# A two-part LSTM step reordered on TensorE and VectorE, the SSM's output product in four full-width pieces, and the SSM's input products dealt out 12, 11, 11, 2

## The reference, cut to what matters

```python
h = tanh(x[:, t] @ Wx + b + h @ Wh)                      # layer 0, for each t: x = x + h
B, C = softplus(conv(x) @ Wp[:, :64] + .), tanh(conv(x) @ Wp[:, 64:] + .)   # layer 1
u = x @ Ws + bs
state = decay * state + dt * B * u                       # for each t
x = x + (C * state) @ Wo + bo
A = x[:, t] @ Wx + b + h @ Wh                            # layer 2, for each t; Wh is 512 x 2048
i, f, o = sigmoid(A[:512]), sigmoid(A[512:1024]), sigmoid(A[1024:1536]); g = tanh(A[1536:])
c = f * c + i * g
h = o * tanh(c)                                          # x = x + h
x = x + x @ layer                                        # layer 3
```

## Time and profile before

| | |
|---|---|
| median of 3 runs | 4203.66 us (4202.13 to 4208.72) |
| profiled execution, its own time | 4200.99 us |
| span of its trace | 4199.2 us |
| PE busy | 3705.6 us (88%) |
| DVE busy | 3546.8 us (84%) |
| ACT busy | 1392.5 us (33%) |
| POOL busy | 782.9 us (19%) |
| granted TensorE clock, mean | 0.991 |

### The profile page before, as it was taken

How to read it: one execution, slowest core, us unless ns; L and a number is a source line. 1 busy time by engine, 2 the same in 40 slices (tenths; PEclk the granted TensorE clock), 3 DMA queues, 4 the chain that set the end, 5 groups by cost and what they waited for, 6 DMA issues and landing times.

```text
span 4199.2 us, 260237 instructions
## 1 busy us (share of the span) xinstructions
PE 3705.6 (88%) x111058; PEld 3068.5 (73%) x111058; DVE 3546.8 (84%) x21169; ACT 1392.5 (33%) x6196; POOL 782.9 (19%) x3625
## 2 busy tenths in 40 slices
PE   6989999989999899998989989898999989988866
PEld 4677777777777777777777777777777777777654
DVE  5588888888888888888888888888888888888865
ACT  4233333333333333333333333333333333333221
POOL 0111111112111111111111111111111111111111
PEclk9999999999999999999999999999999999999998
DMA  7100000000000000000000000000000000000000
GB/s 257 46 7 7 10 9 9 9 7 7 9 9 9 9 6 6 9 9 9 9 6 7 8 9 9 9 9 6 7 9 9 9 9 6 6 7 7 6 5 7
DMA packets 19102, 63.37 MB, mean 15 GB/s; under 512 B 3958, under 2 KB 4526, under 8 KB 14914
## 3 DMA queue, kind: packets, MB, share of 16 engines
q1 hardware_dynamic: 17692, 46.67, 3.5%
q10 hardware_dynamic: 294, 0.33, 0.0%
HBM read 38.48 MB, written 8.39 MB: 11 GB/s over the span
## 4 chain that ended last, share of the span: by engine, by line
DVE 46%; PE 35%; ACT 12%; issue 7%; DMA 1%; DVEq 0%; SPq 0%; ACTq 0%; POOL 0%; POOLq 0%
PE ps_lstm L995 26%; DVE lstm_sums L731 13%; DVE lstm_arg L737 9%; DVE lstm_h_scaled L760 5%; ACT lstm_gates_2c L487 5%; ACT lstm_tanh_c L492 4%; DVE rnn_h_parts L873 3%; DVE lstm_gates_2c L748 3%; DVE rnn_arg L837 2%; PE ps_rnn L1034 2%; DVE lstm_h_parts L764 2%; DVE lstm_h_parts L768 2%; DVE rnn_h_parts L875 2%; ACT rnn_h L504 2%; PE ps_lstm_in_b L1076 2%
## 5 line engine op out<-in xcount | busy, mean ns | idle before, releaser
L995 PE MATMUL ps_lstm<-lstm_Wh_parts,lstm_h_parts 128*20 128x256 f16 x65472 | 1993.3, 274 | 444.2 <-DVE lstm_h_parts L768 414.2
L995 PEld LDWEIGHTS ps_lstm<-lstm_Wh_parts,lstm_h_parts 128*20 128x20 f16 x65472 | 1499.9, 91 | 910.6 <-DVE lstm_h_parts L768 687.8
L487 ACT ACTIVATE lstm_gates_2c<-lstm_arg 128x32 f32<-128x32 f32 x2048 | 469.6, 229 | 1677.0 <-DVE lstm_arg L737 1677.0
L731 DVE STREAM_TRANSPOSE lstm_sums<-ps_lstm 128x256 f32<-128x256 f32 x2048 | 914.1, 446 | 114.4 <-PE ps_lstm L995 84.9
L348 POOL COPY lstm_sums<-lstm_in 128x32 f32<-128x32 f32 x2048 | 427.1, 211 | 1820.2 <-DVE lstm_arg L737 1813.4
L1034 PE MATMUL ps_rnn<-rnn_Wh_parts,rnn_h_parts 128*20 128x128 f16 x32736 | 641.3, 220 | 36.7 <-DVE rnn_h_parts L875 36.0
L737 DVE TENSOR_REDUCE lstm_arg<-lstm_sums 128x32 f32<-128x96 f32 x2048 | 538.1, 263 | 105.5
L1034 PEld LDWEIGHTS ps_rnn<-rnn_Wh_parts,rnn_h_parts 128*20 128x20 f16 x32736 | 550.6, 92 | 74.1 <-DVE rnn_h_parts L875 55.6
L492 ACT ACTIVATE lstm_tanh_c<-lstm_gates_2c 128x8 f32<-128x8 f32 x2048 | 410.5, 200 | 353.7 <-DVE lstm_gates_2c L748 353.6
L504 ACT ACTIVATE rnn_h<-rnn_arg 128x16 f32<-128x16 f32 x1024 | 221.6, 216 | 752.2 <-DVE rnn_arg L837 752.2
L873 DVE TENSOR_SCALAR rnn_h_parts<-rnn_h 128x16 f16<-128x16 f32 x1024 | 226.4, 221 | 240.5 <-ACT rnn_h L504 239.1
(11 more groups left out here) (182 smaller groups left out, 2740.8 us busy)
## 6 DMA issues: line engine op xcount, KB each, us to landing
layer_plus_2I<-in_L_cond_w SPq DMA_DIRECT2D x16, 1024.0 KB, 5.3
out<-out_rows SPq DMA_DIRECT2D x128, 64.0 KB, 1.9
x_rows<-in_x SPq DMA_DIRECT2D x31, 256.0 KB
lstm_Wx<-in_L_cond_Wh SPq DMA_DIRECT2D x1, 4096.0 KB, 17.3
lstm_Wx<-in_L_cond_Wx SPq DMA_DIRECT2D x1, 4096.0 KB, 13.8
layer_plus_2I<-in_L_cond_Wh SPq DMA_DIRECT2D x1, 1024.0 KB, 8.4
rnn_Wx<-in_L_cond_Wx SPq DMA_DIRECT2D x1, 1024.0 KB, 10.8
lstm_in<-in_L_cond_w SPq DMA_DIRECT2D x1, 1024.0 KB, 9.7
```

The costliest lines, as they stand in the source:

```text
L487: A.activation(gate[h][:, 0:G, :].rearrange("p g q -> p (g q)"), arg[h][:, :, :].rearrange("p g n -> p (g n)"), ACT.Tanh, scale=gate_scale ...
L731: return mark(V.transpose(tr[h][s % 2][:, :, 0:QC], psL[h][:, 0:HW].rearrange("p (g c) -> p g c", c=QC)))
L995: ins = mm(psL[h][QC * j:QC * j + LO + NB, 0:HW], hls[:, k, :], whl[:, k, h, e, j, :], start=(k == 0 and e == 0), stop=(k == KB - 1 and e ...
```

## The change

In the LSTM step TensorE issues products(1, 0), which needs half 0 of the state alone, in front of its wait for lstm_h_ready1 and in front of products(0, 2) and (0, 3). VectorE's order for one step becomes T0, R0, [SSM piece], T1, P0, R1, C0, O0, TR, P1, H0, A0, C1, B0, O1, A1, H1, RR, B1, [SSM piece], L873, L875. The vector y gets its own zero-padded place for all four sequences (y, 128 x 128), cleared once by GpSimd instead of the two halves of wo2, and is made by two instructions on 64 partitions each; the product with Wo is 4 matmuls of 128 columns. SSM_CUTS deals the 36 products out as 12, 11, 11 and 2.

```diff
--- before.py
+++ after.py
@@ -49,7 +49,7 @@
 HALO_STEP = 14
 OUT_STEPS = [4, 10, 11, 28]
 SSM_MMS = [("u", TAPS - 1, b) for b in range(KB)] + [(c, k, b) for c in "BC" for k in range(TAPS) for b in range(KB)]
-SSM_CUTS = [0, 8, 20, 32, 36]
+SSM_CUTS = [0, 12, 23, 34, 36]
 EXP_STEP = 2
 SERIES_STEP = 3
 CT_STEP = 5
@@ -175,10 +175,11 @@
         o_s = [sb(f"lstm_o_scaled{h}", [P, HB * NB]) for h in range(NH)]
         tc = [sb(f"lstm_tanh_c{h}", [P, HB * NB]) for h in range(NH)]
 
-        zabs, zmax, ez, den, rden, sr, qr, bt, ct, drive, y, pol_a, pol_b, st_ = [
-            stage[:, 3 * 512 + HS * q:3 * 512 + HS * (q + 1)] for q in range(14)]
+        zabs, zmax, ez, den, rden, sr, qr, bt, ct, drive, pol_a, pol_b, st_ = [
+            stage[:, 3 * 512 + HS * q:3 * 512 + HS * (q + 1)] for q in range(13)]
         wpk = stage[:, 6 * 512:10 * 512].rearrange("p (k b c) -> p k b c", k=TAPS, b=KB)
-        wo2 = stage[:, 10 * 512:12 * 512].rearrange("p (h d) -> p h d", h=2)
+        wo2 = stage[:, 10 * 512:11 * 512]
+        y = stage[:, 11 * 512:11 * 512 + TOK].rearrange("p (t n) -> p t n", n=NB)
         states = st_.rearrange("p (t n) -> p t n", n=2)
         st0 = sb("state0", [P, 2])
         spw = sb("softplus_work", [P, 9, 2])
@@ -269,7 +270,7 @@
             sp.dma_start(wp[:, :, :], rows(Wp)).then_inc(d_ssm, 16)
             sp.dma_start(ws[:, :, :], rows(Ws)).then_inc(d_ssm, 16)
             for h in range(2):
-                sp.dma_start(wo2[NS * h:NS * (h + 1), h, :], Wo[:, :]).then_inc(d_ssm, 16)
+                sp.dma_start(wo2[NS * h:NS * (h + 1), :], Wo[:, :]).then_inc(d_ssm, 16)
             sp.dma_start(whl32[:, :, :], rows(l2_Wh)).then_inc(d_lstmw, 16)
             for q in range(W2BUFS - 1):
                 load_w2(q)
@@ -319,10 +320,8 @@
             nc.gpsimd.affine_select(out=ident[:, :], in_=ident[:, :], compare_op=ALU.not_equal, fill=1.0, base=0,
                                     pattern=[[-1, P]], channel_multiplier=1).then_inc(q_id, 1)
             pool.wait_ge(q_id, 2)
-            nc.gpsimd.memset(wo2[NS:P, 0, :], 0.0).then_inc(q_id, 1)
+            nc.gpsimd.memset(y, 0.0).then_inc(q_id, 1)
             pool.wait_ge(q_id, 3)
-            nc.gpsimd.memset(wo2[0:NS, 1, :], 0.0).then_inc(q_id, 1)
-            pool.wait_ge(q_id, 4)
             pool.wait_ge(rmax, 1)
             nc.gpsimd.partition_all_reduce(wmaxa[:, 0:1], wmax[:, 0:1], P, RMAX).then_inc(rmax_all, 1)
 
@@ -751,17 +750,19 @@
                 def out_gate(h):
                     return mark(V.tensor_scalar(o_s[h][:, :], gate[h][:, 2, :], 1.0, H_SCALE, ALU.add, ALU.mult))
 
-                def new_h(h, s, o_at):
+                def tanh_done(h, s, o_at):
 
                     vec.wait_ge(S[f"lstm_tanhc{h}"], s + 1)
                     vec.wait_ge(S["vec_done"], o_at)
-                    o3 = o_s[h][:, :].rearrange("p (b n) -> p b n", b=HB)
-                    t3 = tc[h][:, :].rearrange("p (b n) -> p b n", b=HB)
-                    at = mark(V.tensor_tensor(half(hl, h)[:, :, s, :], o3, t3, ALU.mult))
-                    return at, o3, t3
-
-                def hi_part(h, o3, t3):
-                    return mark(V.tensor_tensor(half(hls, h)[:, :, 0:NB], o3, t3, ALU.mult))
+
+                o3 = [t[:, :].rearrange("p (b n) -> p b n", b=HB) for t in o_s]
+                t3 = [t[:, :].rearrange("p (b n) -> p b n", b=HB) for t in tc]
+
+                def h_part(h, s):
+                    return mark(V.tensor_tensor(half(hl, h)[:, :, s, :], o3[h], t3[h], ALU.mult))
+
+                def hi_part(h):
+                    return mark(V.tensor_tensor(half(hls, h)[:, :, 0:NB], o3[h], t3[h], ALU.mult))
 
                 def lo_part(h, s, at):
                     vec.wait_ge(S["vec_done"], at)
@@ -809,8 +810,13 @@
                         vec.wait_ge(S["vec_done"], m_p[0])
                         vec.wait_ge(S["ct_ready"], 1)
                         mark(V.tensor_copy(st0[:, :], states[:, CT - 1, :]))
-                        V.scalar_tensor_tensor(out=y, in0=st_, scalar=spt[:, 1:2], in1=ct, op0=ALU.mult, op1=ALU.mult
-                                               ).then_inc(S["y_ready"], 1)
+                        if known == 1:
+                            vec.wait_ge(q_id, 3)
+                        for h in range(2):
+                            own = slice(NS * h, NS * (h + 1))
+                            V.scalar_tensor_tensor(out=y[own, :, 2 * h:2 * h + 2], in0=states[own], scalar=spt[own, 1:2],
+                                                   in1=ct.rearrange("p (t n) -> p t n", n=2)[own], op0=ALU.mult, op1=ALU.mult
+                                                   ).then_inc(S["y_ready"], 1)
 
                 def series(out_, in_, c, x_):
 
@@ -848,23 +854,26 @@
                             ssm_stage(s, 0)
                         at = transpose(1, s)
                         p_at = products(0, s)
-                        o_at = out_gate(0)
                         reduce(1, s, at)
                         new_cell(0, p_at)
+                        o_at = out_gate(0)
                         if w["rnn"]:
                             r_at = transpose_rnn(s)
                         p_at = products(1, s)
-                        _, o3, t3 = new_h(0, s, o_at)
+                        tanh_done(0, s, o_at)
+                        h_part(0, s)
+                        at = hi_part(0)
                         new_cell(1, p_at)
-                        at = hi_part(0, o3, t3)
+                        lo_part(0, s, at)
                         o_at = out_gate(1)
-                        lo_part(0, s, at)
-                        _, o3, t3 = new_h(1, s, o_at)
-                        at = hi_part(1, o3, t3)
+                        tanh_done(1, s, o_at)
+                        hi_part(1)
+                        at = h_part(1, s)
+                        if w["rnn"]:
+                            reduce_rnn(s, r_at)
                         lo_part(1, s, at)
                     elif w["rnn"]:
                         r_at = transpose_rnn(s)
-                    if w["rnn"]:
                         reduce_rnn(s, r_at)
                     if w["mid"]:
                         ssm_stage(s, 2)
@@ -1002,13 +1011,13 @@
                             pe.wait_ge(S["lstm_h_ready0"], s)
                         products(0, 0)
                         products(0, 1)
+                        products(1, 0)
                         if s == 0 and p["lstm"]:
                             pe.wait_ge(S_last["lstm_h_ready1"], CT)
                         elif s > 0:
                             pe.wait_ge(S["lstm_h_ready1"], s)
                         products(0, 2)
                         products(0, 3).then_inc(S["lstm_mm0"], 1)
-                        products(1, 0)
                         products(1, 1)
                         products(1, 2)
                         products(1, 3).then_inc(S["lstm_mm1"], 1)
@@ -1099,13 +1108,10 @@
                     elif known in (0, 1) and light(CT * known + s):
                         hold(3)
                     if w["mid"] and s == WO_STEP:
-                        pe.wait_ge(S["y_ready"], 1)
-                        y3 = y.rearrange("p (t n) -> p t n", n=2)
+                        pe.wait_ge(S["y_ready"], 2)
                         for b in range(KB):
-                            x2_ = psX[:, TOK * b:TOK * (b + 1)].rearrange("p (t n) -> p t n", n=NB)
-                            for h in range(2):
-                                last = mm(x2_[:, :, 2 * h:2 * h + 2], wo2[:, h, P * b:P * (b + 1)], y3,
-                                          start=False, stop=(b == KB - 1 and h == 1))
+                            last = mm(psX[:, TOK * b:TOK * (b + 1)], wo2[:, P * b:P * (b + 1)], y.rearrange("p t n -> p (t n)"),
+                                      start=False, stop=(b == KB - 1))
                         last.then_inc(S["wo_mm"], 1)
                     if w["mid"] and L2_STEP <= s < L2_STEP + GB:
                         u = s - L2_STEP
```

## The result

The changed kernel takes 4141.19 us (median of 4 runs, 4140.05 to 4143.03). The kernel before took 4205.72 us beside it. The ratio is 0.985, with a 95% interval from 0.9836 to 0.9863: 1.5% faster. The forecast was 4155 with a range of 4125 to 4190.

What follows compares the result with a forecast made beforehand. No engine is full; VectorE and TensorE hand one LSTM step back and forth. Terms of -0.88, -0.02, 0, -0.11 and -0.46 give -1.47 a chunk, 47 us in all: 4201 to 4154, plus 2.7 for the median, 4155; range 4125 to 4190.

Steps and rivals of the forecast that it cites:

- The step: Plain LSTM step, s = 9 and 11 to 31: 3.76 us against 3.80, 0.04 less, 0.88 a chunk.
- RR: VectorE's RNN instruction: at about R1 + 1.43 instead of 1.56, so the RNN no longer matters for T0.
- Both moves are needed: Plain step: the move in TensorE's queue costs 0.07 us, the one in VectorE's gives 0.11.
- The slower rival: T1 waits for R0's end: 0.08 us more in each of about 1000 steps, 80 us, 4235; chance 0.06.
- The wait for lstm_h_ready1: Rival: B1 behind RR comes so late that TensorE stalls inside half 0; 4195 with a 0.04 stall; chance 0.07.
- Steps 5 to 8: Steps with an SSM instruction between R0 and T1: 0 for the four, bounds -0.16 and +0.44 us.
- y: Second VectorE instruction for y once a chunk, up to 0.28 us: counted 0, or 5 us if T0's cover is gone.
- SSM products: New dealing out in TensorE's queue, steps 1 to 4: +0.10, -0.11, 0 and -0.10, sum -0.11 us a chunk.
- Wo: Step 10: four products of 128 columns clear TensorE's full queue, step returns to 3.76, -0.46 us a chunk.
- The loop's top: Step 0: its burst waits for the loop's branch in every second chunk, so only half gain, -0.02 us a chunk.

Runs made afterwards that it cites:

- rr_behind: The changed kernel with RR put back behind B1 in VectorE's order; 4183.02 us, ratio 0.9942, against 4137.8 us for the changed kernel beside it.
- pe_order: The kernel before with TensorE's new order alone; 4271.92 us, ratio 1.0152.
- dve_order: The kernel before with VectorE's new order alone; 4275.48 us, ratio 1.0157.
- stage_moved: The changed kernel with the SSM pieces between R0 and T1 at steps 3 to 8 put behind O1; 4108.22 us, ratio 0.9773.
- y_one: The changed kernel with y made by one VectorE instruction of 128 elements on all partitions instead of two; 4124.4 us, ratio 0.9817.
- both_orders: The kernel before with both new orders, without the changes to y, Wo and the SSM products; 4177.97 us, ratio 0.9921.
- side_only: The kernel before with the new y, Wo and SSM_CUTS, and the old orders on both engines; 4175.16 us, ratio 0.9927.
- after_pad: The changed kernel with four more unused matmuls of 128 columns on TensorE in each chunk; 4159.89 us, ratio 0.9896.

## Why the prediction was right, and where its sum was off

- **The step.** The places on the path of the reckoned step were found within 0.01 us: T0 at burst + 1.32, T1 0.73 behind it, B0 at R1 + 0.94 (0.93), the burst at 1.16 (1.15). Only T1 to R1 is 0.54 instead of 0.56. By the medians a step wins 0.048 instead of 0.04, which makes 5 of the 7 us between -27 and -33.8.
- **RR.** The prediction counted RR at R1 + 1.43 instead of 1.56, so that the RNN no longer holds T0; it is at 1.45. `rr_behind` shows that this was needed and not a side effect: at 1.65 it costs 45 us. The prediction gave no price for it.
- **Both moves are needed.** This is shown by `pe_order` and `dve_order`, which are 66 and 69 us slower.
- **The slower rival** wanted T1 to wait for the end of R0. The gap from R0 to T1 is 0.18 in the changed kernel too, with R0 taking 0.26. The Trainium skill ("VectorE: DVE Perf Modes", section The DRAIN you can't avoid) says that the next op does not start until the pipe is empty, and adds in the same paragraph that one that is not held starts earlier. The prediction took up the first sentence alone; the rows agree with the second, so read whole the section doesn't speak for this rival.
- **The wait for lstm_h_ready1** did not appear: the burst takes 1.93 as before. It was closer than reckoned. B1 is at R1 + 1.57 by the median instead of 1.53, so TensorE hears of it at 1.79 and needs it at 1.82: 0.03 to spare instead of 0.06.
- **Steps 5 to 8** were counted as 0 and cost 4.4 us. The bounds held this. The step of the sum that is off is the guess that the RNN had held T0 anyway: this is true for s = 5 and 6 (-1.4 and -0.1 us), and not for 7 and 8 (+2.8 and +3.1 us). `stage_moved` shows that what stands between R0 and T1 is paid in full.
- **y** was counted as 0, with 5 us as its bound, and costs 3.1 + 1.2 = 4.3 us, which `y_one` gives back as 4.9. The Trainium skill (same page, section Two Vector instructions with no wait between them) says that an instruction whose operands start in another group of 32 partitions than the one before is held until the earlier ones have finished. The rows agree: 0.59 for two, and L882 held though its input was ready.
- **SSM products.** Steps 1 to 4 together gave -5.1 us against -3.4. Step 1 gave -0.1 where +3.1 was counted (its median did rise, from 3.804 to 3.854), and step 4 gave -2.2 where -3.1 was. Undoing the edit costs 7 us in the steps' sums.
- **Wo.** Step 10 gave -15.0 us against -14.3.
- **The loop's top** is the term that the sum lacked. I had noted step 0 as set by the loop's branch and left it as it was. It gave 12.5 us more than I had counted, more than the whole difference between 47 and 58. `both_orders`, `side_only` and `after_pad` show that this wait hangs on TensorE's number of instructions in the loop. With this term the forecast would have been 4143. Nothing in the prediction asked for it, so this part of the gain came by luck.

## What to carry to other kernels

When two engines hand a step back and forth, write the step down as offsets from two points, and add up a move on one engine together with the move on the other that makes room for it: here each alone made the kernel 1.5% slower. Then look at what stands in the queue in front of the instruction that has newly become late (here the SSM pieces in front of T1). What was partly hidden before is now paid in full, and moving it into a wait (here the one for the tanh of cell 1) was worth another 32 us.
